# Base-first order of the selector columns in three graph aggregations

## The reference

```
hb = jnp.einsum('nd,bdo->bno', h, basis)
coef = comp[etypes]
m = coef[:, 0, None] * hb[0][src]
for b in range(1, basis.shape[0]):
    m = m + coef[:, b, None] * hb[b][src]
m = m * norm[:, None]
agg = jax.ops.segment_sum(m, dst, num_segments=n)
out = agg + bias + h @ loop_w
```

## Time and profile before

| | |
|---|---|
| median of 3 runs | 3440.08 us (3434.08 to 3444.99) |
| profiled execution | 3439.91 us |
| its span, first to last instruction | 3438.6 us |
| mean granted TensorE clock | 0.971 |
| busy over the span | PE 91%, DVE 64%, ACT 41%, POOL 36% |
| L0a, steps | 50 to 396 us, the turns until 417 |
| L0b, steps | 597 to 882 us |
| L1, steps | 1016 to 1346 us, last turns until 1359 |

### The profile page before, as it was taken

The page is one execution under the profiler, slowest core; times in us unless marked ns, Lnnn a source line. Parts: engine busy times, 40 slices in busy tenths (PEclk is TensorE's granted clock), DMA queues, the critical chain, the costliest instruction groups (busy, mean ns, idle before and its releaser), DMA issues.

```text
span 3438.6 us, 42149 instructions
## 1 busy us (share of the span) xinstructions
PE 3117.6 (91%) x14851; PEld 2230.3 (65%) x14872; DVE 2186.7 (64%) x4808; ACT 1408.4 (41%) x2135; POOL 1254.6 (36%) x1035
## 2 busy tenths in 40 slices
PE   5899898998978788999998999999999999999998
PEld 2333476444752235866446988778977898778987
DVE  6989522788347774243455768756785576657776
ACT  6888733000341013333144545334542455325544
POOL 3666335777357774442201012411223111331022
PEclk8999998999999999999999999999999999999999
DMA  3555442767337764223102011220012101130012
GB/s 83 161 160 166 131 149 70 215 198 202 86 99 210 210 200 137 79 82 131 40 26 75 7 35 34 70 68 13 32 46 89 40 7 62 43 95 7 7 62 73
DMA packets 137281, 318.29 MB, mean 93 GB/s; under 512 B 25380, under 2 KB 43108, under 8 KB 136046
## 3 DMA queue, kind: packets, MB, share of 16 engines
q0 software_dynamic: 53040, 173.84, 17.7%
q1 hardware_dynamic: 82590, 139.10, 12.8%
q10 hardware_dynamic: 1440, 2.62, 0.2%
HBM read 269.50 MB, written 24.84 MB: 86 GB/s over the span
## 4 chain that ended last, share of the span: by engine, by line
PE 73%; DVE 14%; issue 6%; ACT 3%; DVEq 2%; DMA 1%; POOL 1%; SPq 1%; POOLq 0%; ACTq 0%
PE bank L140 15%; PE bank L142 15%; PE bank L141 15%; PE bank L792 10%; PE bank L2274 5%; DVE G L913 4%; PE bank L802 3%; PE bank L1992 2%; PE bank L1636 2%; PE bank L770 1%; DVE y_tile L1944 1%; DVE y_tile L1946 1%; DVE x_stats L1927 1%; DVEq L861 1%; ACT G L779 1%
## 5 line engine op out<-in xcount | busy, mean ns | idle before, releaser
L792 PE MATMUL bank<-gathered,selector 128*128 128x512 f32 x1326 | 668.0, 619 | 130.8 <-DVE G L913 88.9
L913 DVE TENSOR_TENSOR G<-G,bank 128x512 f32 x663 | 453.8, 684 | 167.9 <-PE bank L792 94.8
L792 PEld LDWEIGHTS bank<-gathered,selector 128*128 128x128 f32 x1326 | 217.7, 193 | 423.6 <-issue 369.1
L1301 POOL TENSOR_TENSOR weight_parts<-weight_ring,weight_parts 128x512 fp32r<-128x512 f32 x136 | 201.3, 1481 | 392.9 <-ACT weight_parts L1273 392.9
L2346 ACT CAST probT<-bank 128x512 fp32r<-128x512 f32 (+1 forms) x480 | 216.2, 524 | 270.5 <-PE bank L2274 270.5
L1289 DVE TENSOR_TENSOR lhs_parts<-G,lhs_parts 128x640 fp32r<-128x640 f32 x128 | 107.2, 838 | 340.4 <-ACT lhs_parts L1271 340.2
L2420 DVE CUSTOM_DVE_ANT_0 prob<-bank,count_by_src 128x512 f32<-128x512 f32 (+1 forms) x480 | 258.4, 588 | 91.3 <-PE bank L142 91.3
L779 ACT COPY G<-bank 128x512 f32<-128x512 f32 x160 | 81.2, 654 | 546.7 <-PE bank L770 546.7
L818 ACT ACTIVATE sign_src<-node_iota_16bit,src_float 128x1280 bf16<-128x1280 f16 x208 | 282.3, 1361 | 49.4 <-PE bank L802 43.6
L140 PE MATMUL bank<-weight_parts,lhs_parts 128*128 128x512 f32 x680 | 271.6, 399 | 33.6 <-POOL weight_parts L1301 30.9
L2352 DVE TENSOR_TENSOR probT<-bank,probT 128x512 fp32r<-128x512 f32 (+1 forms) x480 | 258.9, 595 | 53.6 <-ACT probT L2346 53.6
(11 more groups left out here) (278 smaller groups left out, 6902.1 us busy)
## 6 DMA issues: line engine op xcount, KB each, us to landing
weight_ring<-in_L_gnn_basis SPq DMA_DIRECT2D x64, 256.0 KB, 2.7
weight_ring<-in_L_gnn_bases SPq DMA_DIRECT2D x64, 256.0 KB, 2.6
x_L<-x_rows SPq DMA_DIRECT2D x50, 256.0 KB, 4.5
x_rows<-x_L SPq DMA_DIRECT2D x40, 256.0 KB, 2.0
yT_hi<-yT_new_hi SPq DMA_DIRECT2D x4, 2560.0 KB, 10.8
yT_lo<-yT_new_lo SPq DMA_DIRECT2D x4, 2560.0 KB, 10.9
count_rows<-count SPq DMA_DIRECT2D x10, 640.0 KB, 6.6
count_by_dst<-count_rows SPq DMA_DIRECT2D x10, 640.0 KB, 8.9
```

The source lines that it names most:

```text
L792: pe.matmul(bank[s % banks][:], sel[:, s % SELECTORS, :], xs[:, s % slots, :], start=True, stop=True).then_inc(*multiplied.inc())
L913: dve.tensor_tensor(g, g, bank[s % banks][:], ALU.add).then_inc(*added.inc())
```

## The change

Within a window the pair's position becomes base * nodes + node. Both instructions keep their operands, types and number of elements; what changes is the order in which the elements are run through. In `select` the innermost run is over the nodes, 32 or 16 elements, in which `same` and `sel` are contiguous and `co` stands still. In `take`, where the partitions of G have become columns, ScalarE reads runs of 32 or 16 neighbouring columns of the bank in place of every fourth or eighth column. It writes G in the same order as before: for a base, 128 nodes in a row. The numbers that `transform` reads are in the same places as before. No instruction is added, removed or moved on any engine, and no wait changes.

```
--- before
+++ after
@@ take(j), on ScalarE
             for q in range(nbk):
-                ins = act.copy(G[:, j * nb:(j + 1) * nb, k * P + q * 4 * path.nodes:k * P + (q + 1) * 4 * path.nodes],
-                               bank[first_bank(n) + q][:].rearrange("p (m b) -> p b m", b=nb))
+                nodes = G[:, j * nb:(j + 1) * nb, k * P + q * 4 * path.nodes:k * P + (q + 1) * 4 * path.nodes]
+                ins = act.copy(nodes.rearrange("p b (w n) -> p b w n", n=path.nodes),
+                               bank[first_bank(n) + q][:].rearrange("p (w b n) -> p b w n", b=nb, n=path.nodes))
             ins.then_inc(*taken.inc())
@@ select(i), on VectorE
         dve.tensor_tensor(
-            sel[:, at:at + n, :].rearrange("p t (n b) -> p t n b", b=nb),
-            same[:, 0:n, :].rearrange("p t (n b) -> p t n b", b=1).to_broadcast([P, n, path.nodes, nb]),
-            co[:, :, first:first + n].rearrange("p (b n) t -> p t n b", n=1).to_broadcast([P, n, path.nodes, nb]),
+            sel[:, at:at + n, :].rearrange("p t (b n) -> p t b n", b=nb),
+            same[:, 0:n, :].rearrange("p t (b n) -> p t b n", b=1).to_broadcast([P, n, nb, path.nodes]),
+            co[:, :, first:first + n].rearrange("p (b n) t -> p t b n", n=1).to_broadcast([P, n, nb, path.nodes]),
             ALU.mult).then_inc(*selected.inc())
```

## The result

| | before | after |
|---|---|---|
| median | 3437.24 us (4 runs, 3434.08 to 3444.99) | 3402.82 us (4 runs, 3398.93 to 3407.64) |
| ratio | | 0.9897, 95% interval 0.9873 to 0.9921 |
| profiled span | 3438.6 us | 3404.4 us |
| mean granted TensorE clock | 0.971 | 0.975 |

The change makes the kernel 1.0% faster: 34.4 us by the medians, 34.2 us between the two profiled spans. Forecast were 3407 us and 32.5 us. The forecast started from the 3440.08 us of three runs; the fourth run moved the median of before to 3437.24.

The account below looks back on a forecast made before the run. VectorE was taken to pace L0a, with TensorE bounding late L0b and most of late L1, and GpSimd's gathers limiting earlier L1. Savings of 16 + 9.5 + 7 = 32.5 us gave 3407 us from 3440.08, range 3395 to 3425.

Parts of the forecast that it names:

- The selector's price: Selector's second instruction on VectorE, all three loops: from 1016 to 1053 ns down to 690 ns.
- 57 us off VectorE: VectorE's busy time over the three loops falls by 57 us; called the wrong sum, since each loop has a next bound.
- L0a, 16 us: Loop L0a: 0.34 us saved in each of 49 batches, 16.7 us, less some jitter, so 16.
- L0b, 9.5 us: Loop L0b: 0.33 us at each of 29 TensorE waits before 838 us, nothing after; 9.5 us taken.
- L1, 7 us: Loop L1: some 4 us until 1248 us, where gathers set the pace, and 2.5 to 3 after; together 7.
- The lag part: L1 to step 180: the add's lag behind its gather falls from 9.7 to about 5.8 us, some 4 us gained.
- The copies, 0: ScalarE's copies from PSUM in `take`: 0 us change; best case 0.8 us gained, worst 28 us lost.
- The rest, 0: Outside the loops: no change in the turns behind L0a; same durations from 1359 us on, only shifted.
- The unmoved price: Rival, selector: the price lies in the three-level pattern or broadcast, not the jump; gain 0, 3440 us; chance 0.08.
- the dearer and the cheaper copies: Rivals, ScalarE's copies: dearer by jumps between runs, above 3440 us, chance 0.03; cheaper by 0.1 us each, 3399 us, 0.02.
- Half arrives: Rival, all loops: half of L0a and L0b and 4 us of L1 arrive; 17 us, 3423 us; chance 0.12.
- More arrives: Rival, all loops: 17.5 us in L0a, 13 in L0b, 11 in L1; 41.5 us, 3398 us; chance 0.05.

Follow-up runs that it names:

- e4_table: Kernel before, with only the coefficient table laid out partition x step x base, order of selectors and copies kept: ratio 0.9953 (0.9926 to 0.9980).
- second pair: Kernel before and changed kernel, both unchanged, profiled again on a fourth chip: 3402.82 us changed against 3437.54 before, ratio 0.9893.
- f2: Repeat of e4_table, the kernel before with only the table's layout changed: ratio 0.9943 (0.9924 to 0.9962).

## Why the prediction was right

- *The selector's price.* 690 ns forecast, 691 to 692 measured. The reasoning from L869, an instruction of the same form in the same loop, held. e4_table shows the cause by itself.
- *57 us off VectorE.* It is 17 + 17 + 22.5. That this is not the gain was the main point, and it holds: 34.
- *L0a, 16 us.* 18.1, and 22.3 in the second pair. The batch went by 0.31 us (5.96 to 5.65), and TensorE's wait at the loads by 0.33 (1.94 to 1.61). By the estimate above 15.5 and 15.9 us of it are the batches, which is the forecast's 16. The rest, 2.6 and 6.4 us, are the falls of the granted clock that the kernel before has and the changed one has not. The prediction had no term for the clock; that the total fits is in this part luck.
- *L0b, 9.5 us.* 8.4 and 9.5 (283.6 to 275.2; 284.8 to 275.3). Counting the places in which TensorE waited, and not the batches, gave the right size, 29 x 0.33. It is not shown to be the right reason: TensorE's waits for adds went from 17.9 us in 29 places to 11.1 in 23 (576 to 817 us), 6.8 less and not 9.6.
- *L1, 7 us.* 5.3 and 5.6. The lag part was right: 9.7 to 5.2 forecast as about 5.8, worth 4.0 us. The part after step 180 was mis-sized: 2.5 to 3 forecast, 1.2 came (from the add of step 180 to the last, 99.4 us before and 98.2 after). TensorE has its work there, and the waits for adds were small: 5.2 us in 10 places from 1248 us on, 2.7 in 4 after.
- *The copies, 0.* In L1 they are 591 ns in both. The Trainium skill's rule on PSUM lines ("Advanced Engine Details and Errata", PSUM Cachelines), which would have made them cheaper, does not show in ScalarE's reads: 591 ns strided, 591 in runs of 16.
- *The rest, 0.* 2.4 us came from elsewhere: 3.1 less between L0a's loop and the first gather of L0b (204.6 and 201.5, turns included), 0.9 less before L0a and between L0b and L1, 1.6 more behind L1. The second pair had 0.5 less and 3.6 more in the first and the last of these. I take it as the scatter of a run. The forecast's sum is right by 0.7 us in the loops (31.8 against 32.5; 37.4 in the second pair), because L0a gave 2.1 more by the clock and the other two 2.8 less: that closeness is luck.
- *Rivals.* The unmoved price falls by 691 ns, the dearer and the cheaper copies by 591. "Half arrives" is what the cure by the table's layout gave on the chips with the stalls (15 and 17 us by the medians of e4 and f2), and for a reason that the trace of before could not show. "More arrives" had the right number for L0a alone (17.5), and not by its reason.
- *Not foreseen:* that the clock would add to L0a, and that on other chips the parts in L0b and L1 are worth nothing that can be measured.

## What to carry to other kernels

An operand of a VectorE instruction that jumps 832 or 988 bytes with every element costs half of the instruction's time again, and two cures are equal (no run tried a smaller jump): let the loop over the jumping dimension be an outer one, or lay the table out so that it is the innermost. Look for it by comparing the duration of an instruction with that of others of the same size and type in the same loop.

What the shorter instruction is worth is read from who waits for it: count the waiting places and their length, and then ask for the next bound (here TensorE's 1.40 us a step, its 29 waits, GpSimd's 1.25 us a gather). The same 0.33 to 0.36 us was worth 18 us in the first loop (some 15.5 by the batches, the rest by the clock), 8 in the second and 5 in the third. Two runs of one kernel whose loop differs by some us are worth a look at the granted clock in short windows, and not only at its mean.

## What the runs showed of the hardware that was not expected

- A jump of 832 bytes costs 342 or 325 ns on 512 float32 elements (1034 against 692, 1016 against 691), one of 988 bytes 362, and 368 in an output (1052 against 684): 0.63 to 0.72 ns per element. Four or eight neighbours read over and over cost nothing (691 and 692 ns).
- In L0a TensorE's granted clock fell to its lower level behind a wait of 1.94 us, with TensorE busy in between: behind two and four of the twelve such waits in the two profiles of the kernel before. Each fall made the interval 1.3 to 1.7 us longer.
- Between chips the same kernel differed by 2.8% (3437 against 3532 us), and nearly all of it lies in two loops: with the selectors of before L0b takes 284 or 285 us on the one kind and 313 to 318 on the other, L1 334 and 392 to 399. L0a, a loop with the same gathers, matmuls and adds, is the same within the scatter with the selectors of before (343 to 348 us on both); with the short ones it is 325 on the one kind and 330 to 334 on the other. What L0b and L1 have in common and L0a has not: their rows are gathered from tensors that the kernel itself wrote, `same` lies in PSUM, and TensorE uses three banks. The packets of the gathers do not differ: by their queue's share of the span their mean is 180 to 184 ns in all the profiles. Which of it brings the stalls was not tried.
